# One ScalarE exponential over 2048 columns in place of two over 1024, in a two-stage attention kernel

## The reference

```
x = x + window_attention(group_norm(x))   # shifted 8x8 windows, 16 heads of 16 channels, cosine attention
x = x + axial_attention(group_norm(x))    # along columns and along rows, linear: no softmax
```

## Time and profile before

| | kernel before |
|---|---|
| runs, us | 935.17, 937.96, 937.98 |
| profiled execution, us | 934.75 |
| its span, us | 933.0 |
| TensorE matmul busy, us (share) | 845.5 (91%) |
| VectorE busy | 723.9 (78%) |
| ScalarE busy | 661.1 (71%) |
| GpSimd busy | 486.3 (52%) |
| mean granted TensorE clock, share of full speed | 0.964 |
| exponentials (line 765): operations, mean ns | 64, 1059 |

### The profile page before, as it was taken

The page is one execution under the profiler, slowest core; times in us unless marked ns, Lnnn a source line. Parts: engine busy times, 40 slices in busy tenths (PEclk is TensorE's granted clock), DMA queues, the critical chain, the costliest instruction groups (busy, mean ns, idle before and its releaser), DMA issues.

```text
span 933.0 us, 46002 instructions
## 1 busy us (share of the span) xinstructions
PE 845.5 (91%) x20128; PEld 663.0 (71%) x20128; DVE 723.9 (78%) x1557; ACT 661.1 (71%) x1106; POOL 486.3 (52%) x361
## 2 busy tenths in 40 slices
PE   3356899999999999999999999999999999999765
PEld 2244667777777787787777777778777777786554
DVE  3666788988888888889888888888888888886421
ACT  2235677877787777778778877777877887777541
POOL 5023565565556556555655655655555566555420
PEclk9877999999999999999999999999999999999977
DMA  6100234334433433444444343344444433333443
GB/s 172 43 11 4 46 72 81 76 78 89 91 82 79 90 80 78 82 90 90 88 89 89 75 85 79 78 88 83 88 91 88 90 77 76 78 72 74 90 83 80
DMA packets 334158, 74.04 MB, mean 79 GB/s; under 512 B 282356, under 2 KB 333446, under 8 KB 333958
## 3 DMA queue, kind: packets, MB, share of 16 engines
q1 hardware_dynamic: 333958, 71.11, 37.0%
HBM read 12.31 MB, written 8.40 MB: 22 GB/s over the span
## 4 chain that ended last, share of the span: by engine, by line
PE 81%; SPq 7%; DVE 4%; issue 3%; ACT 2%; DMA 2%; POOL 1%; POOLq 0%; DVEq 0%; ACTq 0%
PE ps L454 22%; PE ps L547 16%; PE ps L606 9%; PE ps L594 6%; PE ps L578 6%; PE ps L475 4%; SPq L404 4%; PE ps L595 3%; PE ps L501 3%; PE ps L511 3%; PE ps L492 3%; SPq L396 2%; PE ps L640 2%; PE ps L630 1%; PE ps L619 1%
## 5 line engine op out<-in xcount | busy, mean ns | idle before, releaser
L909 POOL TENSOR_TENSOR kv<-kv,kv 128x1024 f16<-128x1024 f32 x64 | 136.9, 2139 | 98.9 <-ACT kv L717 96.2
L765 ACT ACTIVATE probs<-probs 128x1024 f32<-128x1024 f32 x64 | 67.8, 1059 | 101.1 <-DVE probs L1154 98.7
L594 PEld LDWEIGHTS ps<-q,gram_wide 128*128 128x128 f16 x2048 | 107.5, 96 | 14.2 <-issue 6.7
L594 PE MATMUL ps<-q,gram_wide 128*128 128x32 f16 x2048 | 111.3, 177 | 5.9 <-DMA gram_wide<-gram 5.0
L914 POOL TENSOR_TENSOR stat<-stat,small 128x2 f32<-128x2 f32 x64 | 43.0, 689 | 136.8 <-DVE stat L1068 136.8
L1094 DVE SCALAR_TENSOR_TENSOR gram<-ps,small,gram 128x512 f16<-128x512 f32 x128 | 94.6, 795 | 23.9 <-ACT gram L734 21.0
L595 PE MATMUL ps<-q,gram_wide 128*128 128x16 f16 x2048 | 110.7, 170 | 0.0
L595 PEld LDWEIGHTS ps<-q,gram_wide 128*128 128x128 f16 x2048 | 106.1, 97 | 0.4
L454 PE MATMUL ps<-xn,w_q 128*128 128x256 f16 x768 | 98.4, 280 | 4.5 <-POOL xn L909 4.5
L734 ACT ACTIVATE gram<-ps,small 128x512 f16<-128x512 f32 x128 | 95.3, 816 | 8.6 <-PE ps L578 8.5
L909 POOL TENSOR_TENSOR xn<-xn,xn 128x512 f16<-128x512 f32 x64 | 74.6, 1165 | 49.2 <-ACT xn L754 49.2
(11 more groups left out here) (120 smaller groups left out, 1927.4 us busy)
## 6 DMA issues: line engine op xcount, KB each, us to landing
gram_wide<-gram SPq DMA_DIRECT2D x256, 128.0 KB, 3.2
v_wide<-kv SPq DMA_DIRECT2D x512, 32.0 KB
x_in<-x SPq DMA_DIRECT2D x32, 128.0 KB, 2.4
x_in<-x SPq DMA_DIRECT2D x64, 64.0 KB, 2.3
out<-y_out SPq DMA_DIRECT2D x32, 128.0 KB, 1.9
out<-y_out SPq DMA_DIRECT2D x64, 64.0 KB, 2.0
probs<-L_conv_w_qkv SPq DMA_DIRECT2D x1, 768.0 KB, 5.3
x<-L_conv_w_qkv SPq DMA_DIRECT2D x1, 768.0 KB, 6.9
```

Source lines behind the costliest of these rows:

```text
L594: pe.matmul(dst.rearrange("p (t i) -> p t i", t=2), high, q1[a][:, :, cols], start=True, stop=False)
L765: act.activation(part, part, ACT.Exp).then_inc(probs_ready[g], 1)
L909: return pool.tensor_tensor(dst, whole, high, ALU.subtract)
```

## The change

The two exponentials of an image, each over half of the tile `probs`, become one operation over the whole tile. It waits for both halves of the biased scores. The two semaphores that told TensorE of the halves become one, which `window_den` waits for. The number of exponentials falls from 64 to 32; their columns stay the same. The place in ScalarE's list stays the same.

```diff
-        probs_ready = [sem(f"probs_ready{g}") for g in range(G)]
+        probs_ready = sem("probs_ready")
...
             def window_den(img):
-                reach(pe, probs_ready[1], img)
+                reach(pe, probs_ready, img)
...
-            def probabilities(g, img):
-                reach(act, biased[g], img)
-                part = probs[:, 4 * g:4 * g + 4, :].rearrange("p a n -> p (a n)")
-                act.activation(part, part, ACT.Exp).then_inc(probs_ready[g], 1)
+            def probabilities(img):
+                for g in range(G):
+                    reach(act, biased[g], img)
+                whole = probs[:].rearrange("p a n -> p (a n)")
+                act.activation(whole, whole, ACT.Exp).then_inc(probs_ready, 1)
...
                 for img in there(k - 1):
-                    probabilities(0, img)
-                    probabilities(1, img)
+                    probabilities(img)
```

## The result

The changed kernel took 954.99, 955.48 and 958.00 us (median 955.48) against 937.96: the ratio is 1.0212, interval 1.0185 to 1.0238, which is 17.5 us more. The sum had said 14.35 us more, the forecast was 951.0. The recorded execution took 958.0 us, with a span of 956.2.

The account below looks back on a forecast made before the run. TensorE, busy 91% of the span, was taken as the bound. The terms 12.1 + 1.7 + 0.25 + 0.5 - 0.2 = 14.35 us gave 949.1 from the profiled run or 952.3 from the median; forecast 951, 8-in-10 range 944.5 to 957.

Parts of the forecast that it names:

- the two waits: TensorE's `window_den` would wait 0.15 us for the exponentials, then `window_qk` 0.4 for GpSimd's result, 0.55 late in all.
- The operation's length: ScalarE's joint exponential over 2048 columns would take 1.91 us, bounds 1.70 and 2.12, making later ScalarE work 0.85 late.
- Its start: The joint exponential would start 0.03 us after VectorE's second addition ends, as the second exponential did before.
- The two covers: Lateness hidden before TensorE waits: 0.70 us ahead of `window_den`, 0.30 us ahead of `window_qk`.
- Nothing is carried over but the 0.55: TensorE pays 0.55 us per pattern image, 22 images, 12.1 us; the other 0.30 is absorbed before ScalarE's `token_copy`.
- Images 0 to 3: In the ramp, images 0 and 1 pay 0.85 us each, 1.7 together; images 2 and 3 pay 0.25 together.
- the clock rival: TensorE's clock falls to 1.2 GHz during `window_den` and `window_pv`: 51 us more, about 1000; chance 0.02.
- Images 17 to 21: `window_pv` is held up there, giving 0.58 us more room; 0.1 us each, 0.5 together, bounds 0 and 2.8.
- The long operation: Rival: the joint exponential takes nearer 2.12 us than 1.91, giving 954 to 960 us; chance 0.07.
- ScalarE's fixed time as the bound: Rival: ScalarE sets the pace, so each image gains 0.21 us, 6.7 in 32, giving 928 us; chance 0.03.
- faster streaming: Rival: the joint exponential takes under 1.36 us, only images 0 and 1 pay, about 935.5 us; chance 0.03.
- Transfers: Rival: the transfer chain sets an image's length, hiding TensorE's later start, giving 936.7 us; chance 0.05.

Follow-up runs that it names:

- e2_onewait: The changed kernel with the joint exponential waiting for `biased[1]` alone instead of both semaphores: 954.7 us, ratio 1.0184 to the kernel before.
- e5: The kernel before with its two exponentials cut at 768 columns in place of 1024, the second over 1280: 940.71 us, ratio 1.0035.
- e6: The kernel before with its two exponentials cut at 512 columns in place of 1024, the second over 1536: 944.76 us, ratio 1.0073.
- the second pair of traces: Both kernels unchanged, profiled once more: the kernel before 939.25 us, ratio 1.0011; the changed kernel 955.39 us, ratio 1.019.
- e4_nostagger: The kernel before with its two exponentials over 1024 columns both waiting for `biased[1]`: 957.45 us, ratio 1.0206.
- e12_quarters: The kernel before with each exponential cut into two over 512 columns, four in an image: 940.16 us, ratio 1.0026.
- e7_copyhalf: The changed kernel's joint exponential waiting for `biased[1]` alone, the second half's addition made a copy of the bias: 995.36 us, ratio 1.0617.

## Why the prediction was right about the two waits and short in its size

The two waits of TensorE came where they were forecast and nearly as long. The step that failed is the one behind them, that nothing else of the lateness reaches TensorE.

**The operation's length** (1.91): 1.916. The slope from the copies and the normalised values held for the exponential.

**Its start** (0.03 after the second addition): wrong, 0.09. The prediction counted what the operation waits for and not in how many instructions: the second semaphore has its own. e2_onewait shows 0.03 with one. It is 0.06 in each image, 0.06 x 21 = 1.3 us of lateness by the sum's own rule, though e2_onewait got only 0.7 us back, which its interval can't tell from nothing.

**The two covers** (0.70 and 0.30): right. The scale of e5, e6 and after shows the first; `window_qk` 0.14 late in e6 and 0.61 in after (0.92 - 0.30) the second. With the start mended the two waits give 0.549 per image, as worked.

**"Nothing is carried over but the 0.55 ... it is added once for each image of the pattern"**, with "the other 0.30 are absorbed before": this is the step that failed. The term measured 0.77 to 0.80 in place of 0.55: 0.62 of lateness (0.55 and the 0.06 of the start) and 0.15 to 0.18 in groups that wait for nothing in the list, the second `gram_matmuls` and `scores` above all. At 21 images 0.77 - 0.55 is 4.6 us, more than the whole difference of 17.4 - 14.35; the drain of these two runs hides the rest.

The 0.30 were to be absorbed on ScalarE at `token_copy` (line 722), and there they are: its wait for TensorE shrinks from 0.46 to 0.20 us. But ahead of it in ScalarE's queue stand the squares of queries and keys (line 772, after the change 773), and VectorE waits for them. From the timelines of ScalarE and VectorE, before:

```profile
470.52 1.00 ACT L772 ACTIVATE qk_sq<-ps 128x1024 f32<-128x1024 f32 x1
...
471.56 1.25 DVE L1107 STREAM_TRANSPOSE qk<-qk_sq 128x1024 f32<-128x1024 f32 x1 [1.61 <-ACT qk_sq L772]
```

and after:

```profile
484.64 1.01 ACT L773 ACTIVATE qk_sq<-ps 128x1024 f32<-128x1024 f32 x1
...
487.69 1.02 ACT L722 ACTIVATE kv<-ps 128x1024 f32<-128x1024 f32 x1 [0.20 <-PE ps L547]
...
485.68 1.25 DVE L1107 STREAM_TRANSPOSE qk<-qk_sq 128x1024 f32<-128x1024 f32 x1 [1.61 <-ACT qk_sq L773]
```

Count from the start of `window_qk`, 467.26 before and 481.08 after. The squares start 3.26 us after it before and 3.56 after the change, VectorE's transpose 4.30 and 4.60, and `gram_low(0)`, which follows on VectorE and releases the second `gram_matmuls`, ends 7.12 and 7.45 after it. The group itself starts 7.78 and 7.82 after it. So the 0.30 pass through VectorE and take the margin of that release from 0.66 to 0.37 us. The same shows where the lateness stays under the cover: by the medians of the 20 images, `gram_low(0)` ends 7.14 us after `window_qk` before, 7.36 in e5_split768, 7.43 in e6_split512 and 7.44 after. The prediction looked for covers that run out entirely; this one didn't, and yet the group was longer. Why a pause goes with it stays open, and so does the part in `scores`.

**Images 0 to 3** (1.95 us): 2.6. The list over the whole run shows the start of it:

```profile
PE ps L501 <- ACT probs L766: 13.4, 29, 4.5
PE ps L454 <- POOL xn L909: 11.9, 25, 4.5
```

Of the 13.4 us, 8.9 are the waits of images 0 and 1, against 7.1 in the earlier trace rows: 1.8 more, where 1.7 were forecast for the two. Some of the matmuls behind them ran at a lower clock as well. The windows of these two stretches, of before and of after (the column ahead of the last two is the granted clock):

```profile
60.00:62.50 2.50, 2.50 (x31) 2.25 (x24) 0.92 (x2) 0.63 (x1) 0.80 (x1) 1.00 0.00 0
82.00:90.00 8.00, 8.00 (x114) 6.11 (x107) 4.54 (x6) 2.69 (x4) 3.71 (x3) 0.90 0.01 2
```

```profile
60.00:62.50 2.50, 2.50 (x48) 1.89 (x41) 1.65 (x3) 0.59 (x1) 0.00 (x0) 0.50 0.02 7
82.00:90.00 8.00, 6.81 (x107) 5.17 (x108) 2.63 (x6) 4.05 (x6) 4.86 (x4) 0.68 0.01 3
```

0.50 is the lower level. TensorE's wait ahead of the first stretch had ended later (`window_den` at 57.40, 56.64 before), so the two windows don't hold the same work; but the second pair of traces shows nearly the same (1.00 and 0.90 against 0.50 and 0.71), and a part of the clock rival seems to have held, in the ramp alone. What it cost there is not shown. In the steady windows the clock stayed at 1.00.

**Images 17 to 21** (0.1 each): +1.2 from 16 to 22, where 1.05 was forecast. That is in part luck: the kernel before alone took 156.90 us there in one trace and 158.29 in the other.

**Between the levels.** The sum added to the median is 952.3; I took 951 for the lower run of before. The runs since then centre on 938, so 1.3 of the 4.5 us that are missing from 951 to 955.5 are this choice.

**The rivals.** The long operation falls by 1.916 us and by e4_nostagger, which loses as much without it. ScalarE's fixed time as the bound falls by e12_quarters, faster streaming by the operation's length. Transfers don't set the pace: they are 0.5 us of TensorE's waits between 100 and 860 us.

**The rule on breaking up.** The loss from joining agrees with the Trainium skill, Perfetto Trace Analysis, section Optimizing Scalar/DVE Operations (break an operation up where an unsaturated engine makes bubbles elsewhere). But e12_quarters broke it up further and gained nothing: the halves already met the cover.

## What to carry to other kernels

Before joining two operations of an engine that isn't the bound, find what the first of them overlaps: the price is that overlap less the time from its end to each start that needs it, read for every waiter in the queue and not for the first alone. Then follow the lateness that the covers hide through the other engines' queues, to where it comes back: here a cover that shrank without running out went with 0.12 to 0.18 us more in each image, so a sum of waits alone came out short. Wait for the last of several semaphores alone where order makes the others sure; it is free, though here not worth much.

## What the runs showed of the hardware

**A copy that another engine holds up.** In e7_copyhalf VectorE copies 1024 float32 columns from SBUF to SBUF:

```profile
L1154 DVE COPY probs<-bias_mask x32: 682/2565/2607, 53.5 to 911.1; 128x1024 f32<-128x1024 f32 x32
```

It takes 0.68 us or 2.57, with the median at the slow end. The timelines of VectorE and GpSimd, in two images:

```profile
493.27 0.68 DVE L1154 COPY probs<-bias_mask 128x1024 f32<-128x1024 f32 x1
...
493.57 2.39 POOL L908 TENSOR_TENSOR kv<-kv,kv 128x1024 f16<-128x1024 f32 x1
...
659.90 2.57 DVE L1154 COPY probs<-bias_mask 128x1024 f32<-128x1024 f32 x1
...
659.80 2.12 POOL L908 TENSOR_TENSOR kv<-kv,kv 128x1024 f16<-128x1024 f32 x1
```

Where the copy starts first, it takes 0.68 and GpSimd's subtraction 2.39; where GpSimd starts first, the subtraction takes its 2.12 and the copy ends 0.55 us after it (659.90 + 2.57 = 662.47; 659.80 + 2.12 = 661.92). The Trainium skill, SBUF — State Buffer, section Who interferes with whom, says that such a copy can need a port pair which it shares with GpSimd, and which the one that issues first holds for the whole instruction, and the trace agrees. The addition, which has one operand in PSUM, shows nothing of it: 1.22 to 1.23 us in all 32.

**A second semaphore** on a ScalarE operation cost 0.06 us (0.093 against 0.033 from the addition's end to the start).
